# Rounded pairs for the second half of the condition layer's down products, and an earlier start of the first gelu blocks

## The chip, the cores and the metric

The kernel runs on one core of a Trainium2 chip. A core has a matrix engine (PE), a vector engine (DVE), an activation engine (ACT), a general engine (POOL) and a queue engine (SP) that issues most DMAs; each runs its own list of instructions in order and they wait for each other by semaphores. The metric is the time of one execution on the device in microseconds; the median of the runs counts.

## The reference

1024 tokens of 128 channels (32 sequences of 32) go through two blocks. The first is two mixtures of experts, one behind the other, added to the input:

```python
x = x + ffn(cond(x, cond_64, ...), ...)
# cond: 8 experts of width 64 (top 2) and a shared one of width 128
y_all = einsum('etm,emh->eth', leaky(x @ w_gate) * (x @ w_up), w_down)
y = combine(y_all, topk_w) + (leaky(x @ sw_gate) * (x @ sw_up)) @ sw_down
# ffn: 16 experts of width 64 (top 4 in 2 of 4 groups), silu, and a shared one
```

The second is an attention with 16 heads, a relative position bias (a small network with silu and layer norms on 63 positions) and a layer norm, followed by a mixture of 8 experts of width 512 (top 2, softmax weights):

```python
h = layernorm(x) * ln_g[e] + ln_b[e]
a = gelu(h @ W1[e] + b1[e]);  y = a @ W2[e] + b2[e] + x
out = sum over the 2 chosen e of gate[e] * y
```

## The kernel before

All work is written out by hand: one list per engine, in the order in which that engine runs it. The tokens go in two halves of 512 (s = 0, 1). Experts of width 64 are taken in pairs, so the condition layer has five blocks of 128 hidden columns (four pairs and the shared one), the second layer nine.

**Exact products by rounded parts.** PE has a fast format (f32r) with a rounded operand. The helper `three` multiplies the rounded part and the rest of both factors in three matmuls (L927 high by high, L928 high by low, L929 low by high). The rounded part comes from ACT (`chunk`, L649, for the weights; `copy_hi`, L643, for the tokens), the rest from a subtraction on POOL (`split`, L503) or DVE (`turned`, L1353). Weights are rounded in 16 chunks: 5 for the condition layer, 9 for the second layer (numbers 5 to 13), 2 for the query weights (14 and 15, constants `CH_Q` to `CH_N`).

**The condition layer's end.** PE computes ten units (`up_unit`, two products each); DVE multiplies their halves (L1398) and weighs each pair by its gates (`weigh`, L1448). Then PE forms the down products (L1024) as plain fp32 matmuls, first the five blocks of the first half into bank 6, with gate spreads (L988) in between, then five of the second half into bank 7. DVE copies each half out (`turned`, L1349), ACT rounds it (`copy_hi(2)`, `(3)`), DVE subtracts (L1353), and PE computes the second router's logits (L1033) and goes on with the second layer's 18 units.

**Around it.** On DVE the position network's first norm stands here: its statistics (L1472 to L1476) ahead of the first half's copy, `rp_norm(0)` (L1453, L1455) behind the first half's subtraction. POOL computes its reciprocal root (`position_rstd`, L507 and L508) after chunk 13 and the memset of `k_diag` (L524). ACT does the silu (L684) ahead of `copy_hi(3)`. After the logits come ACT's tanh (L687) and DVE's routing (L1495 to L1542), woven into the second layer's units. SP starts the load of W1 when POOL and ACT have done chunk 13.

**The last stage** has 16 steps (expert, half). `m_up` computes four blocks (three matmuls each) into banks 0 to 3, ACT applies the gelu (`gelu_block`, L866), DVE rounds blocks 0 and 1 (L1767) and ACT blocks 2 and 3 (`gelu_high`, L873), DVE subtracts (L1771), and `m_down` multiplies by W2. Its beginning is interleaved with the end of the attention, tile by tile: DVE's `projected` and `input_normed` (L1699, behind POOL's `both_rstd`, L609 to L612), PE's `out_turn` (L1212, L1214) and `route` (L1220), DVE's routing of a half (`route_half`), ACT's `route_tanh` (L858) and DVE's `gates_half`.

Of the kernel before, what the change touches and what calls it, by code (L numbers as in the profile page):

```python
# [65 lines left out]
def two_layers(nc, a, out):  # L66
# [5 lines left out]
    with ctx:  # L72
# [17 lines left out]
        w_out = sb("w_out", [P, HB, P])  # L90
        w_kv = sb("w_kv", [P, 2 * DH])
        arena2 = sb("arena2", [P, 8192])
        base_bias = sb("base_bias", [P, HEADS, LEN])
# [124 lines left out]
        def bank(n):  # L218
            return ps[:, n, :]
# [8 lines left out]
        chunks += [split_cols(F0, F_BLK, b) for b in range(F_BLK)]  # L228
        chunks += [(lambda w, j=j: w[:, Q0 + j * HW:Q0 + (j + 1) * HW]) for j in range(2)]
        CH_F, CH_Q, CH_N = C_BLK, C_BLK + F_BLK, C_BLK + F_BLK + 2  # L230

# [48 lines left out]
        pe_gate = sem("pe_gate")  # L280
        v_sel = sem("v_sel")
        v_warm = sem("v_warm")
        v_gates = sem("v_gates")
# [167 lines left out]
        def _(pool):  # L451
# [53 lines left out]
            def position_rstd(n, sig):  # L505
# [3 lines left out]
                    .then_inc(pool_rp, 1)  # L509

            small_tables()
            for n in range(CH_N):
                if n == CH_Q:
                    position_rstd(0, 1)
                    position_rstd(1, 4)
                    pool.wait_ge(v_comb, 2)
                split(n)
                if n == C_PAIRS:
                    position_inputs()
                    norm_inputs()  # L520
                    router_inputs()
                if n == CH_Q - 1:

                    pool.memset(k_diag[:, :, :, :], 0.0).then_inc(ready, 1)  # L524
# [113 lines left out]
        def _(act):  # L638
# [30 lines left out]
            for u in range(2 * C_BLK):  # L669
                gate_copy(u)  # L670
                if u == 0:
                    act.wait_ge(v_z, 1)
                    act.activation(r_s[:, :, 0:C_EXP], r_z[:, :, 0:C_EXP], ACT.Exp, scale=0.5).then_inc(act_exp, 1)
                for _ in range((0, 0, 1, 1, 2, 1, 2, 0, 1, 1)[u]):
                    chunk(next(f_chunks))
                if u == 7:
                    for s in range(HALVES):
                        gate_rows_high(0, s, C_EXP)
            for n in f_chunks:
                chunk(n)  # L680
            act.activation(tables[:, 2:3], eps[:, 0:1], ACT.Silu)
            copy_hi(2)
            act.wait_ge(v_rp, 2)
            act.activation(rp_h[:, 1, :], rp_h[:, 0, :], ACT.Silu).then_inc(act_rp, 1)  # L684
            copy_hi(3)
            act.wait_ge(pe_log, 2)
            act.activation(r_s[:, :, :], bank(4)[:, 0:P].rearrange("p (t e) -> p t e", e=F_EXP), ACT.Tanh, scale=0.5)\  # L687
                .then_inc(act_exp, 1)
            def high_w1(e):
                act.wait_ge(ld["w1" if e < M_EXP - 1 else "w1_last"], 16)  # L690
# [195 lines left out]
            for t in range(TILES):  # L886
# [9 lines left out]
                if t == 6:  # L896
                    first_half_logits()
                    act.activation(tables[:, 3:4], eps[:, 0:1], ACT.Gelu)
            route_tanh(0)
            gelu_block(0, 0)  # L900
            gelu_block(0, 1)
            out_turned(TILES - 2)
            gelu_block(0, 2)
# [19 lines left out]
        def _(pe):  # L923
# [91 lines left out]
            for s in range(HALVES):  # L1015
                if s == 1:
                    pe.wait_ge(v_small, 4)
                order = (C_PAIRS, 0, 1, 2, 3)
                for n, b in enumerate(order):
                    if b == C_PAIRS:  # L1020
                        pe.wait_ge(v_hid, C_BLK * (s + 1))
                    else:
                        pe.wait_ge(v_mul, C_PAIRS * s + b + 1)
                    mm = pe.matmul(bank(6 + s), c_down[:, b, :], c_hid[:, b, s * HW:(s + 1) * HW],  # L1024
                                   start=(n == 0), stop=(n == C_BLK - 1))
                    if s == 0 and n < C_PAIRS:
                        spread(0, C_PAIRS + n, C_PAIRS)
# [271 lines left out]
            m_up(1, (0, 1))  # L1299
            route(TILES - 2)  # L1300
            out_turn(TILES - 1)
            m_up(1, (2, 3))
            pe.wait_ge(v_wo, TILES)
# [33 lines left out]
        def _(dve):  # L1337
# [139 lines left out]
            for s in range(HALVES):  # L1477
                dve.wait_ge(pe_down, s + 1)
                turned(s, bank(6 + s), 2)
                if s == 0:  # L1480
                    rp_norm(0)
                    dve.wait_ge(ld["gk"], 64)
                    link(dve.tensor_scalar(f_bias[:, :], f_bias[:, :], 0.5, None, ALU.add))
# [272 lines left out]
            projected(TILES - 1)  # L1756
            gates_half(0)
            input_normed(TILES - 1)

            def split_gelu(k, half):  # L1760

                b = slice(2 * half, 2 * half + 2)
                dve.wait_ge(act_gelu, M_BLK * k + 2 * half + 2)
                if k >= 2:
                    dve.wait_ge(pe_m_down, k - 1)
                if half == 0:
                    dve.tensor_copy(g_hi[:, k % 2, b, :], gelu[:, k % 2, b, :]).then_inc(v_ghi, 1)  # L1767
                    dve.wait_ge(v_ghi, k + 1)
                else:
                    dve.wait_ge(act_ghi, k + 1)  # L1770
                dve.tensor_tensor(g_lo[:, k % 2, b, :], gelu[:, k % 2, b, :], g_hi[:, k % 2, b, :].bitcast(f32),  # L1771
# [91 lines left out]
```

## Time and profile before

| | before |
|---|---|
| median of 3 runs | 264.55 us (264.28 to 265.64) |
| the profiled execution | 263.71 us, its span 261.9 us |
| granted clock of PE, mean | 0.992 |
| PE busy | 246.4 us (94%) |
| DVE busy | 211.8 us (81%) |
| ACT busy | 147.5 us (56%) |
| POOL busy | 105.3 us (40%) |
| the chain that ended last | PE 62%, DVE 17%, POOL 8%, ACT 5% |

All times in the rows are from one profiled execution, counted from the start of its span. A busy PE is not PE at its peak: matmuls overlap, so the distance between two starts tells more than the duration of one. An fp32 matmul shows as two records. In a row of a timeline, the brackets give the engine's idle time before the instruction and what the profile takes to have ended it.

### The profile page before, as it was taken

The numbers are of one execution on the slowest core, as the hardware profiler recorded it, in microseconds if no ns is written. First come the engines' busy times: TensorE is split into PE (matmuls) and PEld (weight loads), VectorE is DVE, ScalarE is ACT, GpSimd is POOL, SyncE is SP. The second block draws the span as 40 slices with busy tenths as digits, with TensorE's granted clock in tenths as the row PEclk, the third lists the DMA queues.
The fourth block names the chain that finished last, engine by engine and source line by source line (L and its number), as shares of the span: only waits on it lengthen the run. The fifth ranks groups of instructions, "written<-read, shape, count | busy, mean of one in ns | idle before, by whom it ended". The sixth has DMA issues, their size and how long they took to land.

```text
span 261.9 us, 5119 instructions
## 1 busy us (share of the span) xinstructions
PE 246.4 (94%) x1848; PEld 196.8 (75%) x1848; DVE 211.8 (81%) x423; ACT 147.5 (56%) x239; POOL 105.3 (40%) x145
## 2 busy tenths in 40 slices
PE   7999999999999969988999999899999999999994
PEld 5877467667899849877687667677788888888884
DVE  7897868976876495889779987799998887888883
ACT  2666423445621454688455354687686677877550
POOL 3799310135581844864456758323220101101000
PEclk9999999999999998999999999999999999999999
DMA  6994510010210001211200000015290000000002
GB/s 169 233 271 80 210 70 0 1 43 1 30 24 0 3 5 49 71 43 43 83 4 3 6 0 0 3 58 185 96 325 26 0 0 4 0 0 0 3 1 81
DMA packets 25178, 14.54 MB, mean 56 GB/s; under 512 B 11969, under 2 KB 21862, under 8 KB 25153
## 3 DMA queue, kind: packets, MB, share of 16 engines
q1 hardware_dynamic: 24608, 13.92, 19.3%
q0 software_dynamic: 544, 0.29, 0.7%
q8 instruction: 15, 0.25, 0.4%
q14 instruction: 11, 0.08, 0.1%
HBM read 13.58 MB, written 0.62 MB: 54 GB/s over the span
## 4 chain that ended last, share of the span: by engine, by line
PE 62%; DVE 17%; POOL 8%; ACT 5%; issue 4%; DMA 2%; SPq 1%; DVEq 0%; ACTq 0%; POOLq 0%
PE ps L927 14%; PE ps L929 14%; PE ps L928 14%; PE ps L1086 5%; PE ps L1024 3%; POOL w_lo L503 3%; PE ps L1052 3%; PE ps L988 2%; DVE arena L1491 2%; ACT arena L747 2%; DVE arena L1699 2%; DVE arena L1681 2%; DMA w_stage<-in_L_cond_w_up 2%; DVE ssum L1672 1%; DVE arena L1643 1%
## 5 line engine op out<-in xcount | busy, mean ns | idle before, releaser
L866 ACT ACTIVATE att_bias<-ps,bias 128x512 f32<-128x512 f32 x64 | 43.5, 689 | 13.2 <-PE ps L929 13.1
L927 PE MATMUL ps<-act_hi,w_hi 128*128 128x512 f32 x120 | 48.3, 403 | 1.7 <-DVE arena L1491 0.9
L928 PE MATMUL ps<-act_lo,w_hi 128*128 128x512 f32 x120 | 47.0, 392 | 0.0
L929 PE MATMUL ps<-act_hi,w_lo 128*128 128x512 f32 x120 | 47.0, 392 | 0.0
L1771 DVE TENSOR_TENSOR g_lo<-att_bias,g_hi 128x1024 fp32r<-128x1024 f32 x32 | 39.9, 1258 | 0.6
L927 PEld LDWEIGHTS ps<-act_hi,w_hi 128*128 128x128 f32 x120 | 22.5, 188 | 8.5 <-issue 3.6
L929 PEld LDWEIGHTS ps<-act_hi,w_lo 128*128 128x128 f32 x120 | 22.5, 188 | 5.0
L928 PEld LDWEIGHTS ps<-act_lo,w_hi 128*128 128x128 f32 x120 | 22.6, 188 | 4.4
L705 ACT ACTIVATE xc<-ps 128x512 f32<-128x512 f32 x18 | 10.8, 599 | 16.0 <-PE ps L929 16.0
L1767 DVE CAST g_hi<-att_bias 128x1024 fp32r<-128x1024 f32 x16 | 12.4, 775 | 8.6 <-ACT att_bias L866 8.6
L1448 DVE TENSOR_TENSOR arena<-arena,ps 128x512 f32<-128x512 f32 x24 | 16.1, 684 | 3.4 <-PE ps L988 3.3
L1086 PEld LDWEIGHTS ps<-f_down,arena 128*128 128x128 f32 x144 | 17.8, 192 | 0.6
L1086 PE MATMUL ps<-f_down,arena 128*128 128x128 f32 x144 | 18.1, 275 | 0.0
L873 ACT ACTIVATE g_hi<-att_bias 128x1024 fp32r<-128x1024 f32 x16 | 17.0, 1061 | 0.5
L531 POOL TENSOR_TENSOR r_big<-w_stage,vec 128x512 f32<-128x512 f32 x8 | 8.3, 1042 | 21.9 <-ACT w_hi L699 10.0
L1247 PEld LDWEIGHTS ps<-w_out,arena 128*128 128x128 f32 x128 | 15.0, 191 | 2.8 <-issue 2.7
L1491 DVE TENSOR_TENSOR arena<-xc,ps 128x512 f32<-128x512 f32 x18 | 12.3, 686 | 5.1 <-PE ps L929 4.6
L1247 PE MATMUL ps<-w_out,arena 128*128 128x128 f32 x128 | 16.3, 281 | 0.0
L597 POOL TENSOR_TENSOR w_lo<-w_stage,w_hi 128x512 fp32r<-128x512 f32 x4 | 5.5, 1369 | 25.1 <-ACT w_hi L828 25.1
L597 POOL TENSOR_TENSOR w2b_lo<-w_stage,w2b_hi 128x512 fp32r<-128x512 f32 x4 | 5.8, 1461 | 23.5 <-ACT w2b_hi L828 23.5
L503 POOL TENSOR_TENSOR w_lo<-w_stage,w_hi 128x256 fp32r<-128x256 f32 (+1 forms) x16 | 12.4, 800 | 6.4 <-ACT w_hi L649 5.1
L820 ACT ACTIVATE arena<-ps,nv_col 128x1024 f32<-128x1024 f32 x8 | 8.9, 1113 | 9.3 <-PE ps L1235 9.2
(281 smaller groups left out, 575.9 us busy)
## 6 DMA issues: line engine op xcount, KB each, us to landing
arena<-gate_m SPq DMA_DIRECT2D x16, 256.0 KB, 4.5
w_stage<-in_L_ffn_W SPq DMA_DIRECT2D x9, 256.0 KB, 2.7
w_stage<-in_L_ffn_W SPq DMA_DIRECT2D x1, 1792.0 KB, 7.8
x_tok<-in_x SPq DMA_DIRECT2D x2, 256.0 KB, 3.2
w_stage<-in_L_ffn_w_gate SPq DMA_DIRECT2D x1, 512.0 KB, 4.9
w_stage<-in_L_ffn_w_up SPq DMA_DIRECT2D x1, 512.0 KB, 6.6
w_stage<-in_L_cond_Wq SPq DMA_DIRECT2D x1, 512.0 KB, 6.4
f_down<-in_L_ffn_w_down SPq DMA_DIRECT2D x1, 512.0 KB, 6.0
```

Source lines behind the costliest of these rows:

```text
L503: pool.tensor_tensor(c(w_lo), c(w_stage), c(w_hi).bitcast(f32), ALU.subtract).then_inc(pool_lo, 1)
L866: act.activation(gelu[:, k % 2, b, :], bank(b), ACT.Gelu, bias=bias1[:, c:c + 1])\
L873: act.activation(g_hi[:, k % 2, 2:4, :], gelu[:, k % 2, 2:4, :], ACT.Copy).then_inc(act_ghi, 1)
L927: pe.matmul(dst, wh, xh, start=first, stop=False)
L928: pe.matmul(dst, wh, xl, start=False, stop=False)
L929: return pe.matmul(dst, wl, xh, start=False, stop=last)
L1086: return pe.matmul(bank(6 + s)[:, t * P:(t + 1) * P], f_hid[:, b, cols], f_down[:, b, :], start=first, stop=last)
L1247: mm = pe.matmul(bank(6)[:, 0:P], att_T[:, t % 2, b, :], w_out[:, b, :], start=(b == 0), stop=(b == HB - 1))
L1448: dve.tensor_tensor(hid[:, q, cols], hid[:, q, cols], bank(4 + i % 2), ALU.mult).then_inc(v_mul, 1)
L1491: dve.tensor_tensor(f_hid[:, b, s * HW:(s + 1) * HW], g_sb[:, n % 2], bank(2 * (n % 2) + 1), ALU.mult)\
L1767: dve.tensor_copy(g_hi[:, k % 2, b, :], gelu[:, k % 2, b, :]).then_inc(v_ghi, 1)
L1771: dve.tensor_tensor(g_lo[:, k % 2, b, :], gelu[:, k % 2, b, :], g_hi[:, k % 2, b, :].bitcast(f32), ALU.subtract).then_inc(v_glo, 1)
```

## The change

1. **Down products of the second half.** They use rounded pairs as well: ACT rounds `c_down` once (after its gate of unit 5) and the five blocks of `c_hid`'s second half, each when it is weighed; POOL subtracts (`down_low`, `hidden_low`), and PE runs `three` for each block, after a wait for both. The new tiles lie where `arena2` lies.
2. **Order around it.** On POOL the six new subtractions and `position_rstd(0, 1)` come ahead of chunks 12 and 13 and the memset. On ACT the load of the silu tables comes ahead of the two query chunks, and the position network's silu behind the tanh. On DVE `rp_norm(0)` moves from behind the first half to behind the second.
3. **Start of the last stage.** ACT runs the first two gelu blocks ahead of `route_tanh(0)`; PE runs block 2 of the second step ahead of `out_turn(7)`; DVE rounds the first two gelu blocks (`first_high(0)`) ahead of `input_normed(7)`. In later steps the order of DVE is as before.

```diff
@@ -89,6 +89,11 @@
         w_kv = sb("w_kv", [P, 2 * DH])
+        with nc.sbuf_tensor("c_high", [P, C_BLK, HW], f32r) as c_high, \
+                nc.sbuf_tensor("c_low", [P, C_BLK, HW], f32r) as c_low, \
+                nc.sbuf_tensor("cd_high", [P, C_BLK, P], f32r) as cd_high, \
+                nc.sbuf_tensor("cd_low", [P, C_BLK, P], f32r) as cd_low:
+            pass
         arena2 = sb("arena2", [P, 8192])
@@ -227,6 +232,7 @@
         chunks += [(lambda w, j=j: w[:, Q0 + j * HW:Q0 + (j + 1) * HW]) for j in range(2)]
+        SHARED_FIRST = (C_PAIRS, 0, 1, 2, 3)
         CH_F, CH_Q, CH_N = C_BLK, C_BLK + F_BLK, C_BLK + F_BLK + 2
@@ -508,10 +518,23 @@
+            def down_low():
+                pool.wait_ge(act_cdhi, 1)
+                pool.tensor_tensor(cd_low[:, :, :], c_down[:, :, :], cd_high[:, :, :].bitcast(f32), ALU.subtract).then_inc(pool_cdlo, 1)
+            def hidden_low(n, b):
+                pool.wait_ge(act_chi, n + 1)
+                h = c_hid[:, b, HW:TOK]
+                pool.tensor_tensor(c_low[:, b, :], h, c_high[:, b, :].bitcast(f32), ALU.subtract).then_inc(pool_clo, 1)
             small_tables()
             for n in range(CH_N):
+                if n == CH_Q - 2:
+                    down_low()
+                    for m, b in enumerate(SHARED_FIRST):
+                        hidden_low(m, b)
+                    position_rstd(0, 1)
                 if n == CH_Q:
-                    position_rstd(0, 1)
                     position_rstd(1, 4)
@@ -673,19 +696,32 @@
                     chunk(next(f_chunks))
+                if u == 5:
+                    act.wait_ge(ld["cd"], 32)
+                    act.activation(cd_high[:, :, :], c_down[:, :, :], ACT.Copy).then_inc(act_cdhi, 1)
                 if u == 7:
                     for s in range(HALVES):
                         gate_rows_high(0, s, C_EXP)
-            for n in f_chunks:
-                chunk(n)
             act.activation(tables[:, 2:3], eps[:, 0:1], ACT.Silu)
+            def hidden_high(b):
+                if b == C_PAIRS:
+                    act.wait_ge(v_hid, 2 * C_BLK)
+                else:
+                    act.wait_ge(v_mul, C_PAIRS + b + 1)
+                act.activation(c_high[:, b, :], c_hid[:, b, HW:TOK], ACT.Copy).then_inc(act_chi, 1)
+            for b in SHARED_FIRST:
+                hidden_high(b)
+                if b in (C_PAIRS, 0):
+                    chunk(next(f_chunks))
             copy_hi(2)
-            act.wait_ge(v_rp, 2)
-            act.activation(rp_h[:, 1, :], rp_h[:, 0, :], ACT.Silu).then_inc(act_rp, 1)
             copy_hi(3)
             act.wait_ge(pe_log, 2)
             act.activation(r_s[:, :, :], bank(4)[:, 0:P].rearrange("p (t e) -> p t e", e=F_EXP), ACT.Tanh, scale=0.5)\
                 .then_inc(act_exp, 1)
+            act.wait_ge(v_rp, 2)
+            act.activation(rp_h[:, 1, :], rp_h[:, 0, :], ACT.Silu).then_inc(act_rp, 1)
             def high_w1(e):
@@ -896,9 +932,9 @@
                     act.activation(tables[:, 3:4], eps[:, 0:1], ACT.Gelu)
-            route_tanh(0)
             gelu_block(0, 0)
             gelu_block(0, 1)
+            route_tanh(0)
             out_turned(TILES - 2)
@@ -1015,15 +1051,21 @@
                     pe.wait_ge(v_small, 4)
-                order = (C_PAIRS, 0, 1, 2, 3)
-                for n, b in enumerate(order):
+                    pe.wait_ge(pool_cdlo, 1)
+                for n, b in enumerate(SHARED_FIRST):
+                    if s == 1:
+                        pe.wait_ge(act_chi, n + 1)
+                        pe.wait_ge(pool_clo, n + 1)
+                        mm = three(bank(7), (cd_high[:, b, :], cd_low[:, b, :]), (c_high[:, b, :], c_low[:, b, :]),
+                                   first=(n == 0), last=(n == C_BLK - 1))
+                        continue
                     if b == C_PAIRS:
-                        pe.wait_ge(v_hid, C_BLK * (s + 1))
+                        pe.wait_ge(v_hid, C_BLK)
                     else:
-                        pe.wait_ge(v_mul, C_PAIRS * s + b + 1)
-                    mm = pe.matmul(bank(6 + s), c_down[:, b, :], c_hid[:, b, s * HW:(s + 1) * HW],
+                        pe.wait_ge(v_mul, b + 1)
+                    mm = pe.matmul(bank(6), c_down[:, b, :], c_hid[:, b, 0:HW],
                                    start=(n == 0), stop=(n == C_BLK - 1))
-                    if s == 0 and n < C_PAIRS:
+                    if n < C_PAIRS:
                         spread(0, C_PAIRS + n, C_PAIRS)
@@ -1298,8 +1340,9 @@
             route(TILES - 2)
+            m_up(1, (2,))
             out_turn(TILES - 1)
-            m_up(1, (2, 3))
+            m_up(1, (3,))
             pe.wait_ge(v_wo, TILES)
@@ -1477,8 +1520,9 @@
                 turned(s, bank(6 + s), 2)
-                if s == 0:
+                if s == 1:
                     rp_norm(0)
+                else:
                     dve.wait_ge(ld["gk"], 64)
@@ -1755,18 +1799,27 @@
             gates_half(0)
-            input_normed(TILES - 1)
-            def split_gelu(k, half):
-                b = slice(2 * half, 2 * half + 2)
-                dve.wait_ge(act_gelu, M_BLK * k + 2 * half + 2)
+            def first_high(k):
+                dve.wait_ge(act_gelu, M_BLK * k + 2)
                 if k >= 2:
                     dve.wait_ge(pe_m_down, k - 1)
+                dve.tensor_copy(g_hi[:, k % 2, 0:2, :], gelu[:, k % 2, 0:2, :]).then_inc(v_ghi, 1)
+            first_high(0)
+            input_normed(TILES - 1)
+            def split_gelu(k, half):
+                b = slice(2 * half, 2 * half + 2)
                 if half == 0:
-                    dve.tensor_copy(g_hi[:, k % 2, b, :], gelu[:, k % 2, b, :]).then_inc(v_ghi, 1)
+                    if k >= 1:
+                        first_high(k)
                     dve.wait_ge(v_ghi, k + 1)
                 else:
+                    dve.wait_ge(act_gelu, M_BLK * (k + 1))
+                    if k >= 2:
+                        dve.wait_ge(pe_m_down, k - 1)
                     dve.wait_ge(act_ghi, k + 1)
```

## Rows read from the trace of the kernel before

**Rows 1.** Busy time by stretch: us, each engine's busy (x records), PEclk, DMA.
```profile
43.20:53.00 9.80, 8.92 (x39) 6.35 (x37) 9.28 (x46) 3.59 (x6) 1.42 (x3) 1.00 0.00 1
...
184.00:256.00 72.00, 72.00 (x312) 58.43 (x313) 62.24 (x76) 50.45 (x67) 8.75 (x6) 1.00 0.13 41
```

**Rows 2.** The chain that ended last, 26 to 38.6 us: start, us, what.
```profile
31.38 5.15 PE ps L1024 x12
...
36.53 1.98 PE ps L1033 x16
```

**Rows 3.** Timeline of ACT, 19 to 34 us: start, us, what, [idle before].
```profile
19.10 0.60 ACT L660 ACTIVATE xc<-ps 128x512 f32<-128x512 f32 x1 [0.46 <-PE ps L929]
...
25.99 0.41 ACT L649 ACTIVATE w_hi<-w_stage 128x256 fp32r<-128x256 f32 x1
...
27.45 1.28 ACT L681 ACT_TABLE_LOAD   x1
...
33.67 0.63 ACT L643 ACTIVATE act_hi<-act_T 128x512 fp32r<-128x512 f32 x1 [4.72 <-DVE act_T L1349]
```

**Rows 4.** Timeline of DVE, 31 to 44 us.
```profile
31.41 0.69 DVE L1448 TENSOR_TENSOR arena<-arena,ps 128x512 f32<-128x512 f32 x1 [0.40 <-PE ps L988]
...
32.19 0.34 DVE L1473 SCALAR_TENSOR_TENSOR rp_early<-rp_early,pos 63x128 f32<-63x128 f32 x1
...
32.99 0.65 DVE L1349 COPY act_T<-ps 128x512 f32<-128x512 f32 x1
...
35.01 0.33 DVE L1453 TENSOR_SCALAR rp_early<-rp_early,rp_mv,rp_sd 63x128 f32<-63x128 f32 x1
...
36.63 0.69 DVE L1349 COPY act_T<-ps 128x512 f32<-128x512 f32 x1 [0.89 <-PE ps L1024]
...
38.86 0.29 DVE L1495 SCALAR_TENSOR_TENSOR r_s<-r_s,f_bias 128x128 f32<-128x128 f32 x1
...
40.06 0.69 DVE L1491 TENSOR_TENSOR arena<-xc,ps 128x512 f32<-128x512 f32 x1 [0.28 <-PE ps L929]
...
43.18 0.69 DVE L1491 TENSOR_TENSOR arena<-xc,ps 128x512 f32<-128x512 f32 x1 [0.48 <-PE ps L929]
```

**Rows 5.** Timeline of POOL, 25 to 34 and 159 to 173 us.
```profile
25.40 0.73 POOL L503 TENSOR_TENSOR w_lo<-w_stage,w_hi 128x256 fp32r<-128x256 f32 x1
...
27.14 1.86 POOL L524 MEMSET k_diag<- 128x2112 f32 x1
...
33.41 0.58 POOL L508 TENSOR_TENSOR rp_sd<-rp_sd,half_neg 63x1 f32<-63x1 f32 x1
...
159.61 1.27 POOL L603 TENSOR_TENSOR act_lo<-act_T,act_hi 128x512 fp32r<-128x512 f32 x1
160.84 1.29 POOL L597 TENSOR_TENSOR w_lo<-w_stage,w_hi 128x512 fp32r<-128x512 f32 x1
...
164.22 0.88 POOL L612 TENSOR_TENSOR rstd<-var,half_neg 128x2 f32<-128x2 f32 x1
...
168.40 0.69 POOL L612 TENSOR_TENSOR rstd<-var,half_neg 128x2 f32<-128x2 f32 x1
...
172.12 1.56 POOL L603 TENSOR_TENSOR act_lo<-act_T,act_hi 128x512 fp32r<-128x512 f32 x1 [3.04 <-ACT act_hi L853]
```

**Rows 6.** Timeline of DVE, 159 to 173 us.
```profile
159.69 1.27 DVE L1699 TENSOR_SCALAR arena<-xc,mv_g,rstd 128x128 f32<-128x128 f32 x1 [1.62 <-POOL rstd L612]
...
169.18 0.35 DVE L1699 TENSOR_SCALAR arena<-xc,mv_g,rstd 128x128 f32<-128x128 f32 x1 [1.08 <-POOL rstd L612]
169.44 0.69 DVE L1767 CAST g_hi<-att_bias 128x1024 fp32r<-128x1024 f32 x1
...
172.44 0.27 DVE L1734 COPY comb_T<-ps 32x128 f32<-32x128 f32 x1
```

**Rows 7.** Timeline of PE, 166 to 184 us.
```profile
166.88 0.47 PE L927 MATMUL ps<-act_hi,w_hi 128*128 128x512 f32 x1 [0.34 <-ACT att_bias L866]
...
183.90 0.47 PE L927 MATMUL ps<-g_hi,w_hi 128*128 128x512 f32 x1 [0.68 <-DVE g_lo L1771]
```

More of the change, by code:

```diff
@@ L281, in two_layers @@
         v_sel = sem("v_sel")
+        act_cdhi = sem("act_cdhi")
+        pool_cdlo = sem("pool_cdlo")
+        act_chi = sem("act_chi")
+        pool_clo = sem("pool_clo")
         v_warm = sem("v_warm")
@@ L1762, in split_gelu @@
                 b = slice(2 * half, 2 * half + 2)
-                dve.wait_ge(act_gelu, M_BLK * k + 2 * half + 2)
-                if k >= 2:
-                    dve.wait_ge(pe_m_down, k - 1)
                 if half == 0:
-                    dve.tensor_copy(g_hi[:, k % 2, b, :], gelu[:, k % 2, b, :]).then_inc(v_ghi, 1)
+                    if k >= 1:
+                        first_high(k)
                     dve.wait_ge(v_ghi, k + 1)
                 else:
+                    dve.wait_ge(act_gelu, M_BLK * (k + 1))
+                    if k >= 2:
+                        dve.wait_ge(pe_m_down, k - 1)
                     dve.wait_ge(act_ghi, k + 1)
```

## The prediction

> **What bounds the kernel now.** I read the busy time by stretch first, then the chain of work that ended last, then the timelines of ACT, POOL and DVE (the vector engine) around the two edits. From 184 to 256 us PE is busy for 72.00 of 72.00 us; its 312 matmul records there take 0.231 us each [rows 1]. So whatever is won or lost before 184 us moves the end one for one. From 43.2 to 53.0 us DVE is busy for 9.28 of 9.80 us and PE is not full [rows 1]: the routing of the second expert layer runs on DVE there and sets the pace. Between the two stand the position network, the queries and the attention, which this change doesn't touch; I let a shift pass through them unchanged.
>
> The down products of the condition layer lie on the chain: 12 records in 5.15 us, 0.429 each, then the router's products [rows 2]. One fp32 product of 512 columns shows as two records, so it costs 0.86 us, and the five of the second half 4.29 us.
>
> **Part A, the rounded pairs, on PE.** Five times three records of 0.231 us make 3.46 us instead of 4.29: 0.83 us less. The first half ends at 31.38 + 0.86 = 32.24, so by PE alone the second would end at 35.7 instead of 36.53.
>
> **What the pairs need.** ACT rounds c_down (640 columns) after its gate of unit 5. A rounding of 256 columns takes 0.41 us and one of 512 takes 0.63 [rows 3], so 640 take some 0.74, against an idle 0.46 before the next gate [rows 3]. The gate comes up to 0.3 us late; the DVE product behind it was queued behind another one anyway. I take 0 for it, 0.2 at most. Later ACT turns to the Silu tables: 26.40, plus the 1.28 us load and a one-column activation, gives 27.8; the first rounding of c_hid ends at 28.45. The last waits for the weighing at 31.41 + 0.69 = 32.10 [rows 4] and ends at 32.8. ACT does not bound it; the two chunks of the query weights that it does in between are wanted a whole layer later.
>
> POOL is tighter. Its split of chunk 12 starts at 25.40 [rows 5]; the change puts its own work ahead of that chunk, so down_low starts there. One subtraction of 512 columns starts 1.23 us after another (159.61, 160.84), and one of 256 takes 0.73 [rows 5]; 640 take some 1.5. It is done at 27.0. The five hidden_low start at 28.5 and follow each other by 1.23: starts 28.5, 29.8, 31.0, 32.2, 33.5, the last one's end at 34.75. PE, which needs 0.69 us a block from 32.24, comes to its last block at 35.0, so POOL and PE arrive nearly together. The second half ends at about 35.8: **0.75 us gained on PE** (0.83 at best).
>
> **What is queued behind it.** On POOL now stand, behind the last hidden_low: position_rstd (0.85 us with its two instructions; the power takes 0.58), chunks 12 and 13 (1.45 us), and the memset of k_diag, 1.86 us, which was done at 29.0 [rows 5]. That ends the chunks at 37.1 and a memset from about 37.2 to 39.1, later if anything ahead of it is held. Chunks 12 and 13 are wanted by units 7 and 8 of the next layer, which starts at 38.5 [rows 2] and takes 1.4 us a unit: hidden. The load of w1 waits for chunk 13 on SP's queue and starts 10 us later, at 37 instead of 27; its first reader, ACT's high_w1, comes at the 13th of that layer's 18 units, beyond 53 us: hidden. SP's next loads wait for chunk 15, as before.
>
> On DVE rp_norm(0), 0.6 us, moves from an idle stretch (35.01, before the copy at 36.63 that had 0.89 us of idle ahead) to behind the second half's subtraction [rows 4]. There it stands ahead of the routing's first step, at 38.86, and ACT's silu behind it stands ahead of the first gate of the next layer. Without anything else this costs 0.6 us on DVE against the 0.75 gained. DVE's idle time takes that back (0.28 before the product at 40.06 and 0.48 before that at 43.18 [rows 4]; both were waits for PE, which is now early). So with free ports the DVE-bound stretch would begin some 0.75 us earlier.
>
> **What holds it up.** The rows show that DVE and POOL are not free of each other. A DVE tensor-scalar of 0.35 us took 1.27 while POOL's subtraction of 159.61 ran, and ended 0.08 us after it; a DVE copy out of PSUM in the middle of the one of 172.12 took 0.27 [rows 5, 6]. POOL's power, 0.69 at 168.40, took 0.88 at 164.22 beside a DVE operation on two SBUF operands [rows 5]. Before the change POOL had only position_rstd to do between 29.0 and the end of this stage. Now five DVE instructions run into it:
> - The scale-and-add at 32.19 (two SBUF operands [rows 4]) is issued within 0.1 us of the border between two hidden_low. Let in at the border it costs nothing; missed, it waits for the next one at 33.5. The copy of the first half (32.99) stands behind it, and so goes to 32.8 or 34.0.
> - act_lo of the first half and f_bias: in the first case they end by 35.7, ahead of PE. In the second they meet position_rstd and chunk 12, and the copy of the second half, 36.63 before, goes to 37.0 instead of 35.85.
> - act_lo of the second half meets chunk 13: 0.1 us.
> - rp_norm's tensor-scalar, issued at 38.1 to 39.1, meets the memset, which ends at 39.3 to 39.6. No row shows a memset beside such an instruction. The cost is 0 if it doesn't hold DVE, and up to 1.86 if it starts just ahead. The nearest row is the same DVE form held by POOL arithmetic to its very end, so I take it as held.
>
> So the routing's first step goes from 38.86 to 39.75 (early case) or 39.95 (late case), +0.9 or +1.1. The 0.76 of idle time takes its part: the product at 43.18 comes at +0.15, or at +0.35, in the late case with PE itself 0.37 late. **Part A: +0.1 to +0.35, taken as +0.2 us.** The gain on PE is spent on DVE.
>
> On this the Trainium skill has a rule (SBUF — State Buffer, "Who interferes with whom"): DVE and GpSimd share one port pair, held for a whole instruction, and a DVE instruction in a two-port mode (tensor_scalar, copy, cast from SBUF) contends with any GpSimd instruction, one with two SBUF inputs only with one that reads SBUF. The rows above agree as far as they go. By its letter the memset holds rp_norm; if that were wrong, part A would come out at -0.8 in the early case.
>
> **Part B, the start of the last stage.** gelu_block(0,0) and (0,1) no longer stand behind route_tanh(0) on ACT. PE stood 0.34 us for the first of them at 166.88 [rows 7]; the second step's blocks start at 166.3, and block 2 goes ahead of out_turn(7), into PE's wait for DVE. That alone gives nothing beyond 184 us, since the wait that decides is PE's at 183.90, 0.68 us, for DVE's g_lo [rows 7]. Ahead of it DVE's timeline has no gap from 169.18 on. first_high(0), the cast of 0.69 us at 169.44, moves ahead of input_normed(7), into an idle 1.08 us [rows 6]: 0.72 less on that chain. But there it starts at 168.1, beside POOL's last both_rstd, whose power (168.40 [rows 5]) input_normed waits for. By the 0.88 against 0.69 of such a power, and half a cast at most, that comes 0.2 to 0.5 late. **Part B: -0.2 to -0.72, taken as -0.35 us.** route_tanh(0) waits for DVE's routing of the first half, which ends after both gelus are over, so gates_half(0), which waits for it on DVE, keeps its time. If instead the gelus were late, input_normed and all of DVE would wait behind them.
>
> **Sum.** +0.2 - 0.35 = -0.15 us. The profiled execution took 263.71 us (span 261.9 and 1.8 around it); with the change it would take 263.55. It lies 0.84 below the median of 264.55, so on the median I say **264.4**.
>
> **The rivals.**
> - The port doesn't matter where I put it (0.2). The memset leaves DVE alone and the scale-and-add slips in at its border: part A -0.8, part B -0.35 to -0.72, -1.15 to -1.5 in all: 263.0 to 263.4. For it: no row shows a held memset. Against: the margin of 0.1 us at 32.2.
> - The pairs don't pay because POOL is late (0.12). If the hidden_low take 1.56 us each, as act_lo at 172.12 did beside DVE [rows 5], the last ends 1.3 us later, at 36.1, and PE at 37.1, +0.6. The DVE chain follows at some +0.8: 265.0.
> - **Slower** (0.08): rp_norm meets the memset's beginning. That happens if POOL is held ahead of it while DVE is not, with the memset starting after 38.2; then it ends at 40.1 or later, the routing's step comes at 40.4 to 41.2, and of +1.5 to +2.3 idle time takes 0.76: +0.8 to +1.6, with part B at 0: 265.3 to 266.1.
> - The forecast, 264.0 to 264.9, has 0.6.
>
> The range holds 8 in 10: most of the faster rival and the POOL one: **263.0 to 265.5**. A measurement of this kernel can tell about 0.5%, 1.3 us, from no change. Faster by more than that (below 263.2) takes half of the faster rival and a little for both parts at their best, 0.12; slower (above 265.9) 0.06; 0.82 between.
>
> **What would show it.** In the profile after: L1024's second half as 15 records in about 3.5 us, ending near 35.8; the copy of the second half at 35.9 or 37.0; the tensor-scalar of rp_norm(0) longer than 1 us, ending with the memset; the first product of the DVE-bound stretch within 0.4 us of 43.18; input_normed(7) at 169.4 to 169.7; PE's wait before m_down(2) still there and ending about 0.35 us earlier than part A alone would have it. Wrong would make it a clock below full in these stretches, a rp_norm of 0.33 us, or a shift that a later stage takes back.

## The result: slower by 1.4%, and the profile after

The changed kernel takes **268.7 us** (267.54 to 269.77, 4 runs) against 264.56 for the kernel before beside it (4 runs): ratio 1.0138, interval 1.0102 to 1.0174. A few executions of any kernel here are some per cent slower; the medians below keep them, the ratios and intervals leave them out. The profiled execution took 268.53 us, its span is 266.7 us and the mean granted clock 0.985; before it was 263.71, 261.9 and 0.992. PE is busy 248.0 us (93%), DVE 215.3 (81%), ACT 151.1 (57%), POOL 114.3 (43%).

DVE's timeline after, the same stretch as [rows 4] (start, duration, instruction, idle before it; L1516 is the scale-and-add, L1392 and L1396 are copy and subtraction of a half, L1527 `f_bias`, L1496 `rp_norm`, L1539 the routing's first step, L1535 the second layer's products):

```profile
32.66 1.47 DVE L1516 SCALAR_TENSOR_TENSOR rp_early<-rp_early,pos 63x128 f32<-63x128 f32 x1
...
34.58 0.65 DVE L1392 COPY act_T<-ps 128x512 f32<-128x512 f32 x1
36.00 2.02 DVE L1396 TENSOR_TENSOR act_lo<-act_T,act_hi 128x512 fp32r<-128x512 f32 x1 [0.77 <-ACT act_hi L666]
37.94 1.35 DVE L1527 TENSOR_SCALAR f_bias<-f_bias 128x16 f32<-128x16 f32 x1
39.33 0.69 DVE L1392 COPY act_T<-ps 128x512 f32<-128x512 f32 x1
40.79 0.69 DVE L1396 TENSOR_TENSOR act_lo<-act_T,act_hi 128x512 fp32r<-128x512 f32 x1 [0.77 <-ACT act_hi L666]
41.40 0.33 DVE L1496 TENSOR_SCALAR rp_early<-rp_early,rp_mv,rp_sd 63x128 f32<-63x128 f32 x1
...
42.29 0.29 DVE L1539 SCALAR_TENSOR_TENSOR r_s<-r_s,f_bias 128x128 f32<-128x128 f32 x1 [0.25 <-ACT r_s L721]
...
44.36 0.69 DVE L1535 TENSOR_TENSOR arena<-xc,ps 128x512 f32<-128x512 f32 x1 [1.15 <-PE ps L965]
...
47.51 0.69 DVE L1535 TENSOR_TENSOR arena<-xc,ps 128x512 f32<-128x512 f32 x1 [0.48 <-PE ps L965]
```

Three DVE instructions take 1.47, 2.02 and 1.35 us; in [rows 4] the scale-and-add took 0.34, and the other two took 0.69 and 0.16 in the kernel before:

```profile
34.41 0.69 DVE L1353 TENSOR_TENSOR act_lo<-act_T,act_hi 128x512 fp32r<-128x512 f32 x1 [0.77 <-ACT act_hi L643]
35.59 0.16 DVE L1483 TENSOR_SCALAR f_bias<-f_bias 128x16 f32<-128x16 f32 x1
```

POOL's timeline has what they ran into:

```profile
28.98 6.30 POOL L528 TENSOR_TENSOR c_low<-arena,c_high 128x512 fp32r<-128x512 f32 x5 [1.59 <-ACT c_high L712]
35.24 0.18 POOL L517 TENSOR_TENSOR rp_sd<-rp_mv,eps_t 63x1 f32<-63x1 f32 x1
35.51 0.58 POOL L518 TENSOR_TENSOR rp_sd<-rp_sd,half_neg 63x1 f32<-63x1 f32 x1
36.07 1.40 POOL L513 TENSOR_TENSOR w_lo<-w_stage,w_hi 128x256 fp32r<-128x256 f32 x2
37.42 1.85 POOL L547 MEMSET k_diag<- 128x2112 f32 x1
```

`act_lo` starts at 36.00, ahead of both chunks, isn't let in ahead of the first (36.07) or between the two (the second starts at 36.76), and ends at 38.02, 0.60 after the memset's beginning. `f_bias`, at 37.94, ends with the memset (39.29 and 39.27). PE's timeline: the pairs run as forecast, then come the first half's logits, and then PE has nothing to do for 2.85 us, until the late copy of the second half:

```profile
35.96 0.40 PE L965 MATMUL ps<-c_high,cd_low 128*128 128x512 f32 x1
36.20 1.03 PE L1075 MATMUL ps<-gk,act_T 128*128 128x96 f32 x8
40.08 1.87 PE L1075 MATMUL ps<-gk,act_T 128*128 128x96 f32 x8 [2.85 <-DVE act_T L1392]
```

Behind the idle time the same eight products take 1.87 us instead of 1.03. Busy time by stretch after (the last three numbers are the granted clock, the DMA share and GB/s; ahead of them the busy time of PE, its weight loads, DVE, ACT and POOL) shows why: the clock goes from its full level of 2.4 GHz to 1.2 GHz for some of each stretch between 40 and 44 us. In the kernel before these stretches all have 1.00.

```profile
38.00:40.00 2.00, 0.00 (x0) 0.00 (x0) 1.97 (x3) 0.00 (x0) 1.26 (x1) 1.00 0.68 135
40.00:42.00 2.00, 1.92 (x9) 1.92 (x10) 1.20 (x4) 0.65 (x2) 0.00 (x0) 0.57 0.94 327
42.00:44.00 2.00, 2.00 (x6) 1.57 (x6) 0.93 (x6) 1.05 (x3) 0.00 (x0) 0.58 1.05 409
44.00:46.00 2.00, 2.00 (x9) 1.35 (x9) 1.42 (x5) 0.60 (x1) 0.00 (x0) 1.00 0.13 47
```

The **start of the last stage** (as in [rows 6]; L1743 is `input_normed(7)`, L1807 `first_high(0)`), DVE, then POOL (in the kernel before and after), then PE's deciding wait:

```profile
173.18 0.69 DVE L1807 CAST g_hi<-att_bias 128x1024 fp32r<-128x1024 f32 x1
174.72 0.35 DVE L1743 TENSOR_SCALAR arena<-xc,mv_g,rstd 128x128 f32<-128x128 f32 x1 [0.85 <-POOL rstd L635]
174.98 2.35 DVE L1824 TENSOR_TENSOR g_lo<-att_bias,g_hi 128x1024 fp32r<-128x1024 f32 x2
```

```profile
168.13 0.19 POOL L611 TENSOR_TENSOR var<-var,mv_g 128x1 f32<-128x1 f32 x1
...
173.17 0.74 POOL L634 TENSOR_TENSOR var<-var,mv_g 128x1 f32<-128x1 f32 x1
173.99 0.69 POOL L635 TENSOR_TENSOR rstd<-var,half_neg 128x2 f32<-128x2 f32 x1
```

```profile
188.71 0.47 PE L963 MATMUL ps<-g_hi,w_hi 128*128 128x512 f32 x1 [0.70 <-DVE g_lo L1824]
```

**Where the 4.8 us of the two spans are.** One execution gets to this stage up to 2.8 us later than another (the DVE instruction named here starts between 29.07 and 31.88 in the undisturbed profiles), so I count every time from its start. It stands ahead of the change: DVE's copy of the small vectors (29.84 us in the kernel before, 30.30 after). From there, in us:

| | before | after | difference |
|---|---|---|---|
| copy of the second half | 6.79 | 9.03 | +2.24 |
| third product of the second layer (43.18 and 47.51) | 13.34 | 17.21 | +3.87 |
| fifth product | 16.80 | 20.65 | +3.85 |
| PE turns the normed tiles of the second half | 66.01 | 69.90 | +3.89 |
| `input_normed(6)` (165.81 and 170.86) | 135.97 | 140.56 | +4.59 |
| end of PE's wait before `m_down(2)` | 154.06 | 158.41 | +4.35 |

So the start-up gives 0.46 us, part A 3.85, something in the attention 0.70, and part B -0.24. The fifth product takes place 10.01 us behind the copy of the second half in the kernel before and 11.62 behind it after: of the 3.85, 2.24 are the late copy and 1.61 lie between the copy and the product, where the clock is low.

### The profile page after: what moved, and what is told of

Read it like the earlier page. It is cut to its first block, busy times and chain, and to the rows that moved or that the text cites. A ratio compares the mean times of both kernels' runs of the same rounds, so it can differ in the third digit from the quotient of the medians.

```text
span 266.7 us, 5148 instructions
## 1 busy us (share of the span) xinstructions
PE 248.0 (93%) x1853; PEld 199.4 (75%) x1853; DVE 215.3 (81%) x423; ACT 151.1 (57%) x245; POOL 114.3 (43%) x151
## 3 DMA queue, kind: packets, MB, share of 16 engines
q1 hardware_dynamic: 24608, 13.92, 19.1%
## 4 chain that ended last, share of the span: by engine, by line
PE 57%; DVE 23%; POOL 8%; issue 5%; ACT 5%; DVEq 0%; ACTq 0%; POOLq 0%
PE ps L963 13%; PE ps L964 12%; PE ps L965 12%; PE ps L1128 5%; POOL w_lo L513 3%; PE ps L1094 2%; PE ps L1024 2%; DVE g_lo L1824 2%; DVE arena L1535 2%; ACT arena L783 2%; PE ps L972 1%; DVE arena L1743 1%; PE ps L1183 1%; PE ps L1066 1%; PE ps L1217 1%
## 5 line engine op out<-in xcount | busy, mean ns | idle before, releaser
L963 PE MATMUL ps<-act_hi,w_hi 128*128 128x512 f32 x120 | 49.0, 408 | 1.3 <-DVE arena L1535 0.8
L1807 DVE CAST g_hi<-att_bias 128x1024 fp32r<-128x1024 f32 x16 | 12.4, 774 | 8.7 <-ACT att_bias L902 8.6
L1535 DVE TENSOR_TENSOR arena<-xc,ps 128x512 f32<-128x512 f32 x18 | 12.2, 685 | 6.0 <-PE ps L965 5.6
```

The source lines that it names most:

```text
L963: pe.matmul(dst, wh, xh, start=first, stop=False)
L1535: dve.tensor_tensor(f_hid[:, b, s * HW:(s + 1) * HW], g_sb[:, n % 2], bank(2 * (n % 2) + 1), ALU.mult)\
L1807: dve.tensor_copy(g_hi[:, k % 2, 0:2, :], gelu[:, k % 2, 0:2, :]).then_inc(v_ghi, 1)
```

## The experiments

Landmarks are those of the table, from one execution each; the times are of all runs. The theory: part A costs what POOL holds DVE for, and then the clock. The rivals: the pairs themselves (ACT, POOL or PE late), the load of W1 that now runs at 38 to 44 us, or part B.

**One part alone.** The pairs with their new order, without the new start of the last stage; and the reverse.

```diff
# a: ACT route_tanh(0) ahead of the gelus again, PE m_up(1,(2,3)) behind out_turn(7),
#    DVE's cast behind input_normed(7); b: only these three, in the kernel before
```

> Part A alone (the start of the last stage as before the change). Theory P (the port: three DVE instructions held by POOL's queue push the second half's copy from 36.6 to 39.3): the whole of the loss is here, 4.0 to 4.8 us over the kernel before, and the copy stands at 39.3 again. Rival Q (part B is what costs, by its cast beside POOL's root): less than 3 us over the kernel before.

> Part B alone on the kernel before. Theory P: -0.2 to -0.3 us against the kernel before (the traces of before and after differ by -0.24 between input_normed(6) and the wait before m_down(2)); POOL's last L611 takes 0.74 instead of 0.19. Rival Q: 0.5 us or more slower than before.

Measured: the pairs alone 268.83 us (ratio 1.0124, 1.0043 to 1.0205), the copy of the second half at 9.06, the fifth product at 22.13; the same three holds (1.49, 2.04, 1.35) and a longer stretch of low clock (0.66, 0.50, 0.50 and 0.63 in the four stretches of 2 us from 38): from the copy to the fifth product it takes 13.07 us, 3.06 more than before. By the ratio the pairs alone cost 1.1 to 5.4 us, which doesn't tell the forecast's 4.0 to 4.8 from the rival's 3; the landmarks do (4.28 us at the end of PE's wait before `m_down(2)`). The gelus alone 265.46 us (ratio 1.0007, 0.9975 to 1.0038), the fifth product at 16.81, and from `input_normed(6)` to PE's wait 17.86 instead of 18.09 us: -0.23, as in the changed kernel. In the traces the loss is all part A's. What part B wins is too small to be timed.

**The memset.** It moves behind POOL's second `low_w1`; all else is as changed. It was run twice; the first has only its times (267.8 us, by the ratio 267.0, forecast 266.2 to 267.5; ratio 1.0087, 1.0039 to 1.0135), since the profiled execution was disturbed.

```diff
-                if n == CH_Q - 1:
-                    pool.memset(k_diag[:, :, :, :], 0.0).then_inc(ready, 1)
             for e in range(6):
                 low_w1(e)
+                if e == 1:
+                    pool.memset(k_diag[:, :, :, :], 0.0).then_inc(ready, 1)
```

> The changed kernel with the memset alone moved behind low_w1(1); chunks 12 and 13 stay behind the hidden_low. Theory P: f_bias takes 0.2 instead of 1.35, act_lo still 2.0; the copy comes at 38.1 instead of 39.3, 1.2 us less on DVE, and a part of the clock's fall with it: 266.2 to 267.5. If the memset doesn't hold DVE: no change, 268.7.

> The changed kernel with the memset alone moved behind the second low_w1; all else as changed. Measured from DVE's copy of the small vectors: if the memset is what makes the copy of the second half late, f_bias takes 0.16 us instead of 1.35 and that copy comes at 7.8 instead of 9.0 us; the two chunks still hold act_lo(0) for 2.0 us, so it can't reach the 6.5 of c_chunks_first. If the memset doesn't hold f_bias, that stays at 1.35.

DVE in the second run (268.64 us, one execution):

```profile
37.41 2.02 DVE L1395 TENSOR_TENSOR act_lo<-act_T,act_hi 128x512 fp32r<-128x512 f32 x1 [0.77 <-ACT act_hi L665]
39.35 0.16 DVE L1526 TENSOR_SCALAR f_bias<-f_bias 128x16 f32<-128x16 f32 x1
39.55 0.69 DVE L1391 COPY act_T<-ps 128x512 f32<-128x512 f32 x1
```

`f_bias` is back at 0.16, `act_lo` is unchanged, and the copy comes at 7.84: **the memset costs 1.19 us** and does so through `f_bias` alone. The fifth product comes at 19.46, earlier by the same 1.19: PE's pause is still 1.66 us, the clock still falls (0.74, 0.50 and 0.91 in the three stretches of 2 us from 40), and the way from the copy to that product still takes 11.62 us.

**The chunks too.** Chunks 12 and 13 go back ahead of the hidden blocks (the memset stays late), so POOL has nothing behind `position_rstd`.

```diff
                 if n == CH_Q - 2:
                     down_low()
+                if n == CH_Q:
                     for m, b in enumerate(SHARED_FIRST):
                         hidden_low(m, b)
                     position_rstd(0, 1)
-                if n == CH_Q:
                     position_rstd(1, 4)
```

> The changed kernel with chunks 12 and 13 ahead of the hidden_low on POOL (it is idle there for 1.6 us) and the memset of k_diag later, behind low_w1(1). Theory P: act_lo of the first half takes 0.7 to 0.9 instead of 2.02, f_bias 0.2 instead of 1.35, the copy comes at 36.9, PE's clock stays full, and the time falls by 3.3 to 3.9 us to 264.8 to 265.4. Rival R (the pairs themselves are late, or PE's clock falls whatever POOL does): it stays above 266.5.

```profile
32.44 1.48 DVE L1515 SCALAR_TENSOR_TENSOR rp_early<-rp_early,pos 63x128 f32<-63x128 f32 x1
...
35.79 0.69 DVE L1395 TENSOR_TENSOR act_lo<-act_T,act_hi 128x512 fp32r<-128x512 f32 x1 [0.77 <-ACT act_hi L665]
36.40 0.17 DVE L1526 TENSOR_SCALAR f_bias<-f_bias 128x16 f32<-128x16 f32 x1
36.60 0.69 DVE L1391 COPY act_T<-ps 128x512 f32<-128x512 f32 x1
```

Both holds behind the first copy are gone (the scale-and-add's 1.48 stays), the copy comes at 6.52, 0.27 ahead of the kernel before, the clock stays at 1.00 and the fifth product comes at 16.55, 0.25 earlier than before. From the kernel with the memset late to this one the copy gains 1.32 us and the fifth product 2.91: the difference is the clock. Measured 265.93 us (by the ratio 265.4, forecast 264.8 to 265.4), ratio 1.0028 (0.9994 to 1.0063); the rival's 266.5 lies above the interval. The pairs are not the trouble; what was queued on POOL beside them is.

**The chunks first, but the memset right behind `position_rstd(0, 1)`.**

> The changed kernel with chunks 12 and 13 ahead of the hidden_low, but the memset still right behind position_rstd(0, 1). Theory P: act_lo takes 0.7 to 0.9, the memset then runs from 36.1 to 38.0 beside f_bias, which is held to its end: the copy comes 1.1 us later than in c_chunks_first and 1.3 earlier than in the changed kernel. With the fall of PE's clock going with PE's idle time, the routing's first product comes 1.3 to 2.5 us earlier than in the changed kernel. If the two chunks alone were the cause, e_chunks_only is as fast as c_chunks_first.

Measured 266.76 us, ratio 1.0066 (1.0041 to 1.0092). DVE, then POOL:

```profile
31.56 3.40 DVE L1514 SCALAR_TENSOR_TENSOR rp_early<-rp_early,pos 63x128 f32<-63x128 f32 x1
...
37.45 0.82 DVE L1525 TENSOR_SCALAR f_bias<-f_bias 128x16 f32<-128x16 f32 x1
```

```profile
28.58 6.24 POOL L528 TENSOR_TENSOR c_low<-arena,c_high 128x512 fp32r<-128x512 f32 x5
...
36.38 1.85 POOL L538 MEMSET k_diag<- 128x2112 f32 x1
```

The run misses its forecast and does not price the chunks: the scale-and-add, issued in the middle of a subtraction, is passed at the borders of 32.30 and 33.55 and gets in when the last of them ends (34.82). With `f_bias` held in part the copy comes at 9.09 and the fifth product at 20.64, as in the changed kernel by another way. The list of POOL is that of the kernel with the chunks first up to this place, but counted from DVE's landmark its first subtraction starts 0.69 us later (-0.63 instead of -1.32 us), and the same scale-and-add takes 3.40 instead of 1.48. So both the place and the amount of a hold depend on where in POOL's run DVE arrives, which can change from one execution to the next.

**The position statistics later.** As the kernel with the chunks first, and DVE does the statistics between the copy of the first half and its subtraction.

```diff
                 dve.tensor_copy(act_T[:, cols], src).then_inc(v_T, 1)
+                if between:          # position_stats, s == 0 only
+                    between()
```

> c_chunks_first with the position network's statistics behind the first half's copy instead of ahead of it. Theory P: the scale-and-add is still held by a hidden_low, but the copy no longer stands behind it: first copy 1.5 us earlier, second copy at the end of PE's products, 0.2 to 0.4 us earlier than in c_chunks_first; the DVE-bound stretch gains 0 to 0.4. Rival: the copy of the second half was never bound by DVE in c_chunks_first, and nothing moves.

Measured 263.65 us, ratio 0.9967 (0.9933 to 1.0000), so no change isn't quite left out. The scale-and-add takes 0.62, the copy of the second half comes at 6.17 and the fifth product at 16.19, 0.61 earlier than before: nearly the 0.75 that the pairs gain on PE. `act_lo` still takes 1.25 beside the last hidden block, in time that DVE would otherwise wait for PE. Its attention had a break of 1.09 us (see below), and at the end of PE's wait before `m_down(2)` it is 0.37 us later than before while the timed runs are 0.9 us shorter: a difference of this size isn't to be read from one execution.

**The clock by itself.** The changed kernel with twelve dummy matmuls between the two halves' logits; DVE's holds stay.

```diff
             second_logits(0)
+            for _ in range(12):
+                pe.matmul(bank(3), w2b_hi[:, 0:P], w2b_hi[:, :], start=True, stop=True)
             second_logits(1).then_inc(pe_log, 1)
```

> The changed kernel with 12 matmuls more (zeros into an unused bank) in PE's idle time ahead of the second half's logits, which keep PE busy. It prices the clock alone. If the granted clock of 0.57 behind 40 us costs what its rows say (logits 1.9 instead of 1.0 us, the first five matmuls at 0.43 instead of 0.23), the first product of the second layer's stretch comes 1.3 to 1.9 us earlier than in the changed kernel, with f_bias and act_lo held as before. If the clock costs nothing, it doesn't move.

```profile
38.00:40.00 2.00, 1.92 (x13) 1.46 (x12) 1.20 (x3) 0.63 (x1) 0.05 (x1) 1.00 0.94 299
40.00:42.00 2.00, 2.00 (x10) 1.61 (x10) 1.85 (x9) 1.07 (x3) 0.00 (x0) 1.00 1.04 403
42.00:44.00 2.00, 2.00 (x10) 1.37 (x9) 1.86 (x7) 0.69 (x2) 0.00 (x0) 1.00 0.46 177
```

Measured 265.32 us, ratio 1.0044 (1.0003 to 1.0084). The copy comes at 9.05, as late as in the changed kernel; the clock stays at 1.00 and the fifth product comes at 19.06 instead of 20.65: **the clock costs 1.59 us**. The mean granted clock is 0.992 to 1.000 in all ten executions, against 0.985 and 0.986 in the four of the changed kernel. The load of W1 fills the same stretches (DMA share 0.94 and 1.04), so it is not what slows PE. The timed runs gain some 2.5 us on the changed kernel by the two ratios, more than the 1.59; part of that may be another fall of the clock, ahead of the attention, which the profiled execution doesn't have (last section).

**Padding.** The kernel with the chunks first and sixteen small matmuls at the start, to see whether the stall in the attention (below) moves with them.

> c_chunks_first with 16 small matmuls more at the start of PE's list, in its wait for x. In every kernel with the pairs PE stood 0.5 to 0.8 us after the 57th of the 64 records of one attention step, in none without them. If that stand belongs to a place in PE's list of instructions (theory L), it comes 16 instructions earlier, after about the 41st record, or the next smaller unit of counting; if it is a wait of that step (rival W), it stays after the 57th. The time is that of c_chunks_first within 0.5 us.

Its runs lie between 263.96 and 275.41 us (271.23 median, 4 runs), so its time tells nothing. Its profiled execution was disturbed too, but the place of the break can be read from it, since that is a count of records:

```profile
134.06 0.82 PE L1218 MATMUL ps<-k_diag,arena 128*32 128x66 f32 x41
135.91 0.55 PE L1218 MATMUL ps<-k_diag,arena 128*32 128x66 f32 x23 [1.03 <-issue]
```

It comes after the 41st record, sixteen earlier, as theory L says.

**A filled pause.** Ahead of the attention PE waits 1.67 us (1.66 in the changed kernel) for the second half's normed tiles and soon after 0.85 us for ACT, and the clock falls behind that. PE's first eight bias products go into this pause, with the late statistics (i) and in the kernel before (j).

```diff
                 if t == 1:
+                    shift_bias(0)
                     turn_tiles(1)
 ...
                     q_rows(t + 2)
-                if t == 1:
-                    shift_bias(0)
```

> f_stats_late with one step more: PE's first eight bias products (L1093, 1.03 us) move from behind q_rows(3) to ahead of the turning of the second half's tiles, into PE's idle time of 1.66 us there. Two ideas. (1) What they fill is idle time, and with a shorter pause the granted clock stays at 1.00 behind it (in f_stats_late it is 0.50 for two stretches of 2 us): the scores then begin some 1.6 us earlier after that place, as in g_hold_clock and a_pairs_only, and some 0.9 us of PE work leaves the stretch; 1.5 to 2 us less than f_stats_late, some 262.0. (2) The attention is bound by DVE and the wait for its query norms, and what PE wins is idle again: the wait before the next queries keeps its time and the kernel stays at 263.6 within 0.4.

> The kernel before with that one move of the bias products and nothing of the change. It tells whether what i_late_and_bias gains belongs to the pairs or to the move: by idea (1) 1.5 to 2 us less than before, some 262.8; by idea (2) no change (264.5). What is left between this kernel and i_late_and_bias is what the repaired pairs are worth: 0.5 to 0.9 us if the landmark of f_stats_late (fifth product 0.61 us earlier than before) holds, and none if it doesn't.

Busy time of i by stretch, from the start of the turning on (97.35 us):

```profile
97.35:99.35 2.00, 1.15 (x6) 0.90 (x7) 1.91 (x3) 1.38 (x2) 1.97 (x2) 1.00 0.44 131
99.35:101.35 2.00, 2.00 (x7) 1.46 (x7) 1.68 (x4) 0.97 (x3) 2.00 (x3) 0.53 0.00 0
101.35:103.35 2.00, 2.00 (x14) 2.00 (x12) 2.00 (x2) 1.32 (x2) 1.02 (x1) 0.62 0.00 0
```

Measured: i 263.81 us against 264.6 (ratio 0.9944, 0.9906 to 0.9982), j 263.59 (ratio 0.9964, 0.9922 to 1.0007). Idea (1) fell in its main point: with the pause down from 1.66 to 0.81 us the clock still goes to 0.53 behind it (0.51 in j), and the scores begin only 0.9 us earlier (19.83 instead of 20.69 us after the start of the turning). In j most of that is lost again ahead of a value product (0.97 us instead of 0.39; the profile says the softmax, but see below). The time is the one that idea (2) gave for i. The kernel i is faster than the kernel before by 0.2 to 0.9%, the only faster one whose interval leaves out no change; that it is faster than j isn't shown.

## Why the prediction was wrong, point by point

**What the pairs need, and their gain.** Right. 15 records from 32.13, 0.68 to 0.69 us a block in the middle, the last block at 35.43, the second half's end at 36.20, which is 35.74 in the time of the kernel before (0.46 less, as all below); forecast 35.8. ACT and POOL keep up: down_low took 1.56 us, the five hidden blocks 6.30.

**The scale-and-add.** The late case came. It was issued at 32.66, the next subtraction began at 32.68, and it got in at the next border: the copy of the first half at 34.12 (forecast 34.0).

**The failed step: "they meet position_rstd and chunk 12, and the copy of the second half ... goes to 37.0".** It went to 38.87. I had let a held instruction in at the next border. `act_lo` was passed ahead of chunk 12 (36.07) and between the chunks (36.76) and waited for both: 0.68 us, the difference between 7.84 in the kernel without the memset and the 7.16 of the forecast. Then `f_bias`, 0.16 us of work that I had ended before the copy and so before the memset, met the memset: 1.19. Together 1.87, as 38.87 - 37.0 says. The costliest rival ended at 266.1 us, so the range had no place for it.

**The memset.** "I take it as held" was right of a DVE tensor-scalar, and wrong of which one. `rp_norm` took 0.33 at 41.40, after the memset. The slower rival ("rp_norm meets the memset's beginning") named the mechanism and put it on the wrong instruction, with the wrong condition (POOL held and not DVE), and so at 0.08.

**The clock.** No term of the sum, only the last sentence of what would make it wrong. PE's first logits end at 36.8 and my late case ends the copy at 37.7, a pause of 0.9 us. The kernel with the chunks first has one of 0.34 and keeps a clock of 1.00; no run has one of 0.9 at this place. With the copy at 38.87 it is 2.85 us, and the clock's 1.59 come on top, a term that I had put at nothing. The sum closes: 0.37 (the late case's own delay of the copy) + 1.87 + 1.59 = 3.83, measured 3.85 at the fifth product and 3.87 at the third. From the other side: copy 9.03 to 6.52 and the clock, 2.51 + 1.59 = 4.10, is the distance of the fifth product to that of the kernel with the chunks first (20.65 to 16.55).

**"I let a shift pass through them unchanged."** Wrong by 0.70 us in these two traces. In the attention PE stops 0.82 us inside one group of scores, for nothing that the profile names, and from that group's start to the product behind it the shift grows from 3.97 to 4.57:

```profile
127.20 1.05 PE L1217 MATMUL ps<-k_diag,arena 128*32 128x66 f32 x57
129.07 0.32 PE L1217 MATMUL ps<-k_diag,arena 128*32 128x66 f32 x7 [0.82 <-issue]
```

Every kernel with the pairs has it, seven records ahead of the group's end and 0.52 to 1.09 us long; with twelve more matmuls ahead it comes nineteen ahead of the end (0.96 us), with sixteen more 23 ahead (1.03 us). Counted from the start of PE's list it is the same place in all nine profiles, behind 808 matmul records. So it belongs to a place in PE's list of instructions. It is not new with the pairs, though the matmul rows of the kernels without them show no such break. Two records further, at the value product that follows the group, those rows name a wait for the softmax. The weight loads tell more: in j PE makes the first of them when the softmax is there and then stops for 0.72 us, with the gelus alone for 0.47, and in the kernel before the eight loads take 0.47 us instead of 0.21. The rows of j:

```profile
123.83 0.13 PEld L1234 LDWEIGHTS ps<-arena,v_tok 32*64 32x64 f32 x1 [0.29 <-DVE arena L1680]
124.67 0.20 PEld L1234 LDWEIGHTS ps<-arena,v_tok 32*64 32x64 f32 x7 [0.72 <-issue]
```

From the group's start to the product behind it the kernels without the pairs take 1.52 (before), 1.84 (the gelus alone) and 2.10 us (j), those with them 1.82 to 2.39. So how much of the 0.70 the change causes, and how much is this stop's own spread, isn't shown. Why PE stops stays open; in all twelve profiles a transfer of 16 KB by the DMA queue that the profile calls instruction starts 2.2 to 2.7 us before PE goes on, which fits a late load of instructions but doesn't prove it (in the changed kernel it starts at 126.53; queue, transfers, MB and share from 126 to 128 us):

```profile
q8 instruction: 1, 0.02, 3.0%
```

**Part B.** Right: -0.24 us (forecast -0.2 to -0.72, taken as -0.35). The cost was put on POOL's power; it fell on the operation ahead of it (0.74 instead of 0.19 us at 173.17, ending with the cast; their starts are 0.01 us apart), and `input_normed(7)` waits 0.85 us behind the cast. It comes 0.49 us late against `input_normed(6)` (forecast 0.2 to 0.5), and the cast's 0.72 are saved behind it: -0.23. In the timed runs this can't be seen.

**What the page said.** The Trainium skill (SBUF — State Buffer, "Who interferes with whom") has a DVE instruction with two SBUF inputs contend only with a GpSimd (POOL) one that reads SBUF, and one in a two-port mode with any. The trace agrees: `act_lo` ran beside the memset (to 38.02, from its beginning at 37.42; with the chunks first and the memset behind it took its plain 0.69 us inside the memset), and `f_bias` waited for its end. The page also says that whoever issues first has the ports for the whole instruction; it does not say that the waiting one can be passed at a border, which five runs show here (2.02 to 2.04 us in the changed kernel, the pairs alone, the memset late and the dummy matmuls, 3.40 with the chunks first and the memset behind).

## What to carry to other kernels

A short DVE instruction on two SBUF operands, or a tensor-scalar from SBUF to SBUF, can cost what POOL still has queued back to back, not only what POOL is doing at that moment: sum POOL's whole run without a gap as the upper end (for the tensor-scalar a memset too), and put such an instruction where the engine that it feeds is late anyway. Where a sum makes PE wait in a new place, look for rows of what the lower clock costs behind a pause (here 1.5 to 1.6 us in three kernels, behind 1.66, 1.73 and 2.85 us of idle time, 3.06 behind 2.87 in a fourth, and nothing behind 0.34). So taking away a part of a pause need not give the clock back: with the memset late the pause was shorter by 1.19 us and the clock cost the same. Matmuls added ahead move the work that stands at a fixed place in PE's list: look at what PE does there, and at the rows of its weight loads before a wait is put down to the engine that the profile names.

## What I had not expected of the hardware

- POOL passed a waiting DVE instruction: chunks 12 and 13 (1.40 us) went ahead of `act_lo`, two subtractions of 1.25 us ahead of the scale-and-add in the kernel with the chunks first and the memset behind. In others it waited for one subtraction alone (32.66 to 34.13 in the changed kernel, where that subtraction began 0.02 us after it). What decides is open.
- In the changed kernel a memset of 2112 columns (1.85 us) held a DVE tensor-scalar of 0.16 us to its end (1.35).
- The granted clock behind the same pause of 1.67 us ahead of the attention was 0.50 for a stretch of 2 us in most profiles and 1.00 in two (the pairs alone, and the dummy matmuls), whose scores began some 1.5 us earlier (19.1 instead of 20.4 to 20.7 us after the pause). It isn't the kernel alone that decides: of 19 executions of the kernel before, two had a mean clock of 1.00 (262.31 and 262.61 us), the others 0.975 to 0.994 (263.38 us and more). What decides, the runs don't show.
